# Inter-chunk and state products of the mixer in three rounded matmuls, their operands split on three engines

## Chip, cores and metric

The kernel runs on one core of one Trainium2 chip. The metric is the device time of one execution in microseconds. The engines are TensorE (PE in the rows, PEld its weight loads), VectorE (DVE), ScalarE (ACT), GpSimd (POOL) and SyncE (SP), which issues the DMAs.

## What is computed

A two-layer model on 1024 tokens of width 512: a Mamba-like mixer, a 4-bit quantised SwiGLU, a small attention over heads within a token, and a routed low-rank layer. The change is in the mixer. Its reference, cut to what matters (64 heads of 64 in 8 groups, state width 128, a causal conv of 4 taps):

```python
proj = einsum('bld,pd->blp', hidden_states, in_proj_w)      # gate, x, B, C, dt
xBC = silu(causal_conv(hbc, conv_weight) + conv_bias)       # x, B, C
dt_p = softplus(dt + dt_bias); dA = exp(dt_p * A)
def step(state, inp):
    state = state * dA_t[..., None, None] + dtx_t[..., None] * B_t[:, :, None, :]
    y_t = einsum('bhpn,bhn->bhp', state, C_t)
y = ys + x * D
yn = y * rsqrt(mean(y * y) + EPS) * norm_weight * silu(gate)  # mean over a group
x = x + einsum('bli,di->bld', yn, out_proj_w)
```

The final state is not an output of the whole program.

## The kernel before

The recurrence is computed in chunks of 128 tokens: 8 groups of heads, and in each group 8 chunks c = 0 to 7 (n = 8g + c counts them all). Per chunk, `y` is the sum of an intra-chunk part (`em`, the masked decay matrix times B and C, with `x_dt`), an inter-chunk part (C with the `state` left by the chunks before, scaled by `ecum`) and `x_d`. The state becomes its decayed self (`state_dec`) plus the state product, B with the weighted x (`x_w`).

Most products are taken with operands split into a rounded part and a rest (`_hi`, `_lo`, type fp32r): `three_pass` runs hi x hi, hi x lo and lo x hi into one PSUM bank. The inter-chunk product (L904, into `p_in`) and the state product (L909, into `p_x`) are plain fp32 matmuls, which the profile shows as two matmul records each.

Each engine has a fixed order of work written out by hand, with semaphores between them. In chunk c:
- TensorE: transposes of x into `p_x` (L872), transposes of the last chunk's z into `p_in` (L835), `p_gb` (B transposed, and B with C), the decay product into `p_d0` and `p_d1` (L888), the first conv tile into `p_tile` (L84 and L88), the output product of the last chunk into `p_y`, the inter-chunk product, the state product, in chunks 0, 1, 4 and 5 a second conv tile into `p_d1`, the intra-chunk product into `p_y` (L920), and the next chunk's gate product. It makes the conv tiles of the half sequence ahead; the last group has none from chunk 4 on, and takes the gate product in their place.
- ScalarE: the silu of a conv tile left over, `xs` from `p_x` (L471), `zt_hi` from `p_in` (L453), the exponentials `em` (L477) with a table load ahead, the read of `p_tile` into `conv` (L444), roundings of the next group's weights (L433, L436), the tile's silu (L449) with a table load, the square sum of y (L495), the silu of the gate (L459), which waits until z is done.
- VectorE: `gm` and `b_tok` from `p_gb`, `zt_lo` (L578), `em` times `gm` (L660), two taps of the conv tile (L558), the residual, which adds the last chunk's `p_y` into `x_res` (L586) and so frees `p_y`, the other taps, `y` from `p_in` (L684), the state (L690, L692), `y` plus `p_y` (L701), `z` (L710), taps of the second tile.
- GpSimd: `state_dec` (L365), `x_w` (L371), `x_dt` (L374), `g_rstd` (L401), `x_d` (L379), rests of weights `w_lo` (L407), `y` plus `x_d` (L390).

TensorE's intra-chunk product waits for `em` (`s_m`), for `x_dt` and for the residual of the chunk before (`s_res`). The inter-chunk product waits for the state (`s_stu`) and for `zt_lo` (`s_zlo`), since `p_in` holds z transposed.

```python
pe.wait_ge(s_m, 2 * (n + 1))
pe.wait_ge(s_xdt, n + 1)
wait(pe, s_res, n)
for h in range(HG):
    mm = pe.matmul(p_y[:, h * HD:(h + 1) * HD], em[:, c % 2, h * P:(h + 1) * P],
                   x_dt[:, h * HD:(h + 1) * HD], start=True, stop=True)
```

Of the kernel before, what the change touches and what calls it, by code (L numbers as in the profile page):

```python
# [14 lines left out]
F32 = mybir.dt.float32  # L15
# [8 lines left out]
P = 128  # L24
# [67 lines left out]
def mixer(nc, io, ctx, x_res, ident, mean_var2, rstd2, q_prep):  # L92
# [5 lines left out]
    def sb(name, shape, dt=F32):  # L98
        return ctx.enter_context(nc.sbuf_tensor(name, shape, dt))
# [4 lines left out]
    def sem(name):  # L104
        return ctx.enter_context(nc.semaphore(name))
# [17 lines left out]
    em = sb("em", [P, 2, HG * P])  # L123
    b_tok = sb("b_tok", [P, P])
    xs = sb("xs", [P, 2, GW])
# [57 lines left out]
        sem(f"act_{k}") for k in ("xs", "e", "cin", "xc", "sg", "zhi", "ss", "whi"))  # L183

    s_head = sem("ve_head")
    s_gm, s_m, s_tap, s_zlo, s_res, s_t, s_y, s_z, s_stu, s_v, s_wloo = (
# [52 lines left out]
    def by_head(ap):  # L239
        return ap.rearrange("p (h d) -> p h d", h=HG)  # L240
# [116 lines left out]
    def _(pool):  # L357
        def group(g, last):
            for c in range(NC):
                n = g * NC + c  # L360
                st = g * (NC - 1) + c
                if c > 0:

                    pool.wait_ge(s_stu, n)
                    pool.tensor_tensor(by_head(state_dec[:]), by_head(state[:]), heads(ETOT, c), ALU.mult)\  # L365
                        .then_inc(s_std, 1)
                if c == 0:
                    pool.wait_ge(s_head, 5 * (g + 1))
                pool.wait_ge(s_xs, n + 1)
                wait(pool, s_stn, n)  # L370
                pool.tensor_tensor(by_head(x_w[:]), by_head(xs[:, c % 2, :]), heads(DTW, c), ALU.mult)\  # L371
                    .then_inc(s_xw, 1)
                wait(pool, s_intra, n)
                pool.tensor_tensor(by_head(x_dt[:]), by_head(xs[:, c % 2, :]), heads(DT, c), ALU.mult)\  # L374
                    .then_inc(s_xdt, 1)
                if not (isinstance(g, int) and n == 0):
                    norm(n - 1, (c - 1) % 2)
                wait(pool, s_y, n)
                pool.tensor_tensor(by_head(x_d[:]), by_head(xs[:, c % 2, :]),  # L379
                                   d_g[:].unsqueeze(2).broadcast_to([P, HG, HD]), ALU.mult)\  # L380
                    .then_inc(s_xd, 1)
                splits = () if last else SPLIT_IN.get(c, ())
                for w in splits:
                    if w in POOL_LO:
                        w_rest(g + 1, w)
                if c > 0:

                    pool.wait_ge(s_t, st)
                    pool.wait_ge(s_xd, n + 1)
                    pool.tensor_tensor(y[:, c % 2, :], y[:, c % 2, :], x_d[:], ALU.add).then_inc(s_txd, 1)  # L390
# [36 lines left out]
    def _(act):  # L427
# [33 lines left out]
        def group(g, last):  # L461
            for c in range(NC):
                n = g * NC + c
                first = isinstance(g, int) and n == 0
                left, now, later = conv_tiles(g, last, c)
# [78 lines left out]
    def _(ve):  # L544
# [89 lines left out]
        def group(g, last):  # L634
# [7 lines left out]
            for c in range(NC):  # L642
# [9 lines left out]
                ve.tensor_tensor(gm, p_gb[:, 0:P], tri[:], ALU.mult).then_inc(s_gm, 1)  # L652
                ve.tensor_copy(b_tok[:], p_gb[:, P:2 * P]).then_inc(s_gm, 1)
                if not first:
                    z_rest(n - 1)
                ve.wait_ge(s_gm, 2 * (n + 1))
                for k in range(2):
# [20 lines left out]
                if c > 0:  # L678
# [6 lines left out]
                        .then_inc(s_t, 1)  # L685
                ve.wait_ge(s_stn, n + 1)
                wait(ve, s_stu, n)
                if c > 0:
                    ve.wait_ge(s_std, st)
                    ve.tensor_tensor(state[:], p_x[:], state_dec[:], ALU.add).then_inc(s_stu, 1)  # L690
                else:
                    ve.tensor_copy(state[:], p_x[:]).then_inc(s_stu, 1)  # L692
                if c == 0:
# [122 lines left out]
    def _(pe):  # L816
# [44 lines left out]
        def group(g, last):  # L861
            for c in range(NC):
# [5 lines left out]
                if c % CH == 0:  # L868
                    pe.wait_ge(s_xc, (2 * g + c // CH + 1) * TILES - 2)
                wait(pe, s_stu, n)  # L870
                for j in range(GW // P):
# [28 lines left out]
                if c > 0:  # L900

                    pe.wait_ge(s_stu, n)
                    pe.wait_ge(s_zlo, n)
                    pe.matmul(p_in[:], xbc[:, TC, cs], state[:], start=True, stop=True).then_inc(s_inter, 1)  # L904

                pe.wait_ge(s_gm, 2 * (n + 1))
                pe.wait_ge(s_xw, n + 1)
                pe.wait_ge(s_xs, n + 1)
                pe.matmul(p_x[:], b_tok[:], x_w[:], start=True, stop=True).then_inc(s_stn, 1)  # L909

# [987 lines left out]
```

## Time and profile before

| | |
|---|---|
| median of 3 runs | 1382.21 us (1380.33 to 1383.5) |
| the profiled execution | 1379.14 us, its span 1377.3 us |
| busy share of the span | TensorE 94%, VectorE 67%, ScalarE 49%, GpSimd 41% |
| the mixer's groups | from about 66 us to about 1012 us, 119.4 us a group |
| granted TensorE clock in a middle group | 1.00 |

In a middle group the transposes of x mark the chunks: chunk 0 starts at 542.95, chunk 1 at 558.29, chunk 2 at 575.04, chunk 3 at 588.64, chunk 4 at 602.08, chunk 5 at 618.32, chunk 6 at 634.55, chunk 7 at 648.00, and the next group at 662.34. All rows below of such a stretch are of this group. In the rows a time is the start in us from the span's start, then the duration; what stands in brackets is the engine's idle time before the instruction and what ended it. Matmul records overlap, so that the time of a matmul is read from the distance of the starts.

### The profile page before, as it was taken

How to read it: one execution, taken by the hardware profiler on the slowest of the kernel's cores; microseconds unless marked ns; L12 is line 12 of the kernel's file. 1: busy time of each engine (PE TensorE's matmuls, PEld its weight loads, DVE VectorE, ACT ScalarE, POOL GpSimd, SP SyncE). 2: the span in 40 equal slices, each digit the busy share in tenths (PEclk: the TensorE clock that was granted, in tenths of full speed). 3: DMA queues.
4: the chain of work that ended last, by engine and by line, in shares of the span. 5: the costliest groups of instructions: out<-in, count | busy, mean ns of one | idle time of the engine just before them, and what ended most of it. 6: DMA issues, size and time to landing. Idle time of an engine off the chain costs nothing. (4 is left out here: it accounts for less than half of the span.)

```text
span 1377.3 us, 20717 instructions
## 1 busy us (share of the span) xinstructions
PE 1294.3 (94%) x6278; PEld 1011.8 (73%) x6278; DVE 926.7 (67%) x1764; ACT 675.7 (49%) x1055; POOL 564.0 (41%) x567
## 2 busy tenths in 40 slices
PE   5699999999999999999999999999869999879986
PEld 4577877877887787788788778778646766667764
DVE  5876677667667766766766676676656445368995
ACT  3465565566556556656655566655323223222220
POOL 2145345444544534444454444434433333333331
PEclk9899999999999999999999999999979999999997
DMA  5111011011101101100200120000013222131200
GB/s 150 59 47 33 1 59 36 17 33 47 31 1 63 31 16 32 54 24 1 70 24 16 32 62 16 6 28 3 8 41 115 84 77 80 49 100 29 58 16 23
DMA packets 44248, 57.61 MB, mean 42 GB/s; under 512 B 10182, under 2 KB 21156, under 8 KB 43922
## 3 DMA queue, kind: packets, MB, share of 16 engines
q1 hardware_dynamic: 44178, 56.84, 13.7%
q8 instruction: 23, 0.38, 0.1%
q14 instruction: 47, 0.39, 0.1%
HBM read 49.87 MB, written 6.96 MB: 41 GB/s over the span
## 5 line engine op out<-in xcount | busy, mean ns | idle before, releaser
L371 POOL TENSOR_TENSOR x_w<-xs,head_g 128x512 f32<-128x512 f32 x64 | 66.8, 1044 | 296.7 <-ACT xs L471 271.9
L558 DVE SCALAR_TENSOR_TENSOR conv<-p_tile,conv_taps,conv 128x511 f32<-128x511 f32 x189 | 140.7, 745 | 31.7 <-ACT conv L444 22.0
L920 PEld LDWEIGHTS p_y<-x_dt,em 128*128 128x128 f32 x1024 | 123.5, 192 | 26.1 <-issue 22.9
L390 POOL TENSOR_TENSOR y<-y,x_d 128x512 f32<-128x512 f32 x56 | 71.8, 1282 | 165.9 <-DVE y L684 165.9
L660 DVE TENSOR_TENSOR em<-em,p_gb 128x512 f32<-128x512 f32 x128 | 82.2, 683 | 73.6 <-ACT em L477 73.6
L920 PE MATMUL p_y<-x_dt,em 128*128 128x64 f32 x1024 | 121.8, 272 | 4.5 <-DVE x_res L586 4.4
L449 ACT ACTIVATE xbc<-conv 128x512 f32<-128x512 f32 x96 | 60.3, 628 | 130.3 <-DVE conv L566 73.7
L84 PE MATMUL p_tile<-xn_hi,w_hi 128*128 128x512 f32 x252 | 111.2, 441 | 3.2 <-DVE halo L562 3.2
L495 ACT ACTIVATE junk<-y 128x512 f32<-128x512 f32 x64 | 40.5, 633 | 144.3 <-DVE y L701 130.8
L558 DVE SCALAR_TENSOR_TENSOR conv<-p_d,conv_taps,conv 128x511 f32<-128x511 f32 (+2 forms) x99 | 73.9, 746 | 50.7 <-ACT conv L444 46.8
L84 PE MATMUL p_gate<-w_hi,xn_hi 128*128 128x512 f32 x256 | 106.1, 415 | 1.1 <-ACT gate L459 1.1
L84 PE MATMUL p_y<-w_hi,zt_hi 128*128 128x512 f32 x256 | 102.5, 400 | 2.2 <-ACT zt_hi L453 2.2
L407 POOL TENSOR_TENSOR w_lo<-w_raw,w_hi 128x512 fp32r<-128x512 f32 x64 | 82.8, 1309 | 52.5 <-ACT w_hi L433 52.5
L84 PE MATMUL p_y<-w_lo,zt_hi 128*128 128x512 f32 x256 | 102.4, 400 | 0.0
L84 PE MATMUL p_gate<-w_lo,xn_hi 128*128 128x512 f32 x256 | 100.3, 392 | 0.0
L84 PE MATMUL p_tile<-xn_lo,w_hi 128*128 128x512 f32 x252 | 99.3, 394 | 0.0
L477 ACT ACT_TABLE_LOAD x64 | 82.1, 1283 | 1.2
L449 ACT ACT_TABLE_LOAD x61 | 78.3, 1283 | 1.1
L365 POOL TENSOR_TENSOR state_dec<-state,head_g 128x512 f32<-128x512 f32 x56 | 58.4, 1043 | 33.2 <-DVE state L692 33.2
L88 PE MATMUL p_y<-w_hi,zt_lo 128*128 128x512 f32 x256 | 71.1, 400 | 0.0
L1095 POOL TENSOR_TENSOR f_w_lo<-wf,f_w_hi 128x512 fp32r<-128x512 f32 x22 | 30.2, 1374 | 99.7 <-ACT f_w_hi L1136 99.7
L477 ACT ACTIVATE em<-p_d 128x512 f32<-128x512 f32 x128 | 69.6, 596 | 0.7
(293 smaller groups left out, 3316.0 us busy)
## 6 DMA issues: line engine op xcount, KB each, us to landing
w_raw<-w SPq DMA_DIRECT2D x112, 256.0 KB, 2.9
q_words<-q SPq DMA_DIRECT2D x33, 256.0 KB, 2.7
h_ring<-h_lo_rows SPq DMA_DIRECT2D x6, 704.0 KB, 5.0
h_lo_rows<-h_rest SPq DMA_DIRECT2D x11, 256.0 KB, 2.0
x_res<-x SPq DMA_DIRECT2D x8, 256.0 KB, 4.9
out<-out_t SPq DMA_DIRECT2D x8, 256.0 KB, 2.3
h_lo_rows<-h_rest SPq DMA_DIRECT2D x11, 128.0 KB, 1.9
decay_lhs<-cum_parts SPq DMA_DIRECT2D x64, 6.0 KB
```

The lines of the kernel that those rows point to most:

```text
L84: pe.matmul(out, lhs(k)[0], rhs(k)[n], start=(start and k == 0 and n == 0), stop=False)
L88: last = pe.matmul(out, lhs(k)[1], rhs(k)[0], start=False, stop=(k == k_tiles - 1))
L365: pool.tensor_tensor(by_head(state_dec[:]), by_head(state[:]), heads(ETOT, c), ALU.mult)\
L371: pool.tensor_tensor(by_head(x_w[:]), by_head(xs[:, c % 2, :]), heads(DTW, c), ALU.mult)\
L390: pool.tensor_tensor(y[:, c % 2, :], y[:, c % 2, :], x_d[:], ALU.add).then_inc(s_txd, 1)
L407: pool.tensor_tensor(w_lo[:, w, :], w_raw[:, w % RAW, :], w_hi[:, w, :].bitcast(F32), ALU.subtract)\
L449: act.activation(xbc[:, j, half_cols(hf)], conv[:, j % 2, :], ACT.Silu).then_inc(s_xc, 1)
L477: act.activation(em[:, c % 2, k * 512:(k + 1) * 512], p[:], ACT.Exp).then_inc(s_e, 1)
L495: act.activation(junk[:], y[:, c % 2, :], ACT.Square, accum_out=ss[:, c % 2:c % 2 + 1])\
L558: ve.scalar_tensor_tensor(out=conv[:, s, sh:], in0=p[:, 0:HALF - sh], scalar=conv_w[:, bass.ds(g, 1), j, tap], in1=conv[:, s, sh:], op0=AL ...
L660: ve.tensor_tensor(m, m, gm.unsqueeze(1).broadcast_to([P, HG // 2, P]), ALU.mult)\
L920: mm = pe.matmul(p_y[:, h * HD:(h + 1) * HD], em[:, c % 2, h * P:(h + 1) * P], x_dt[:, h * HD:(h + 1) * HD], start=True, stop=True)
```

## The change

The operands of the two products are split into a rounded part and a rest, and each product becomes a `three_pass` of one tile. C and the state and the weighted x are rounded by ScalarE (`c_hi`, `st_hi` behind `zt_hi` and ahead of the exponentials; `xw_hi` behind them), B by VectorE, in place of the copy `b_tok`. The rests are made by GpSimd (`c_lo` ahead of `x_dt`, `xw_lo` behind `g_rstd` and ahead of `x_d`) and VectorE (`b_lo` and `st_lo`, ahead of `em` times `gm`). A group's eighth chunk makes no `x_w`, no state product and no new state, since the next group begins with its own; so chunk 7 of a group no longer decays the state for the chunk behind it either, and the counts of the semaphores follow. The core of the diff:

```diff
--- GpSimd
-                if c > 0:
-                    pool.wait_ge(s_stu, n)
+                if 0 < c < NC - 1:
+                    pool.wait_ge(s_stu, st)
                     pool.tensor_tensor(by_head(state_dec[:]), by_head(state[:]), heads(ETOT, c), ALU.mult)\
                         .then_inc(s_std, 1)
...
+                if c > 0:
+                    pool.wait_ge(s_chi, st)
+                    pool.tensor_tensor(c_lo[:], xbc[:, TC, c * P:(c + 1) * P], c_hi[:].bitcast(F32), ALU.subtract)\
+                        .then_inc(s_clo, 1)
                 wait(pool, s_intra, n)
                 pool.tensor_tensor(by_head(x_dt[:]), by_head(xs[:, c % 2, :]), heads(DT, c), ALU.mult)\
                     .then_inc(s_xdt, 1)
                 if not (isinstance(g, int) and n == 0):
                     norm(n - 1, (c - 1) % 2)
+                if c < NC - 1:
+                    pool.wait_ge(s_xwhi, st + 1)
+                    pool.tensor_tensor(xw_lo[:], x_w[:], xw_hi[:].bitcast(F32), ALU.subtract).then_inc(s_xwlo, 1)
--- ScalarE
                 if not first:
                     z_round(n - 1)
+                if c > 0:
+                    wait(act, s_inter, st - 1)
+                    act.wait_ge(s_xc, (2 * g + c // CH + 1) * TILES)
+                    act.activation(c_hi[:], xbc[:, TC, c * P:(c + 1) * P], ACT.Copy).then_inc(s_chi, 1)
+                    act.wait_ge(s_stu, st)
+                    act.activation(st_hi[:], state[:], ACT.Copy).then_inc(s_sthi, 1)
...
                 for k, p in enumerate((p_d0, p_d1)):
                     act.activation(em[:, c % 2, k * 512:(k + 1) * 512], p[:], ACT.Exp).then_inc(s_e, 1)
+                if c < NC - 1:
+                    act.wait_ge(s_xw, st + 1)
+                    wait(act, s_stn, st)
+                    act.activation(xw_hi[:], x_w[:], ACT.Copy).then_inc(s_xwhi, 1)
--- VectorE
-                ve.tensor_copy(b_tok[:], p_gb[:, P:2 * P]).then_inc(s_gm, 1)
+                ve.tensor_copy(b_hi[:], p_gb[:, P:2 * P]).then_inc(s_gm, 1)
                 if not first:
                     z_rest(n - 1)
-                ve.wait_ge(s_gm, 2 * (n + 1))
+                ve.wait_ge(s_gm, 3 * n + 2)
+                ve.tensor_tensor(b_lo[:], p_gb[:, P:2 * P], b_hi[:].bitcast(F32), ALU.subtract).then_inc(s_gm, 1)
+                if c > 0:
+                    ve.wait_ge(s_sthi, st)
+                    ve.tensor_tensor(st_lo[:], state[:], st_hi[:].bitcast(F32), ALU.subtract).then_inc(s_stlo, 1)
+                ve.wait_ge(s_gm, 3 * (n + 1))
--- TensorE
-                    pe.wait_ge(s_stu, n)
+                    for done in (s_chi, s_clo, s_sthi, s_stlo):
+                        pe.wait_ge(done, g * (NC - 1) + c)
                     pe.wait_ge(s_zlo, n)
-                    pe.matmul(p_in[:], xbc[:, TC, cs], state[:], start=True, stop=True).then_inc(s_inter, 1)
-
-                pe.wait_ge(s_gm, 2 * (n + 1))
-                pe.wait_ge(s_xw, n + 1)
-                pe.wait_ge(s_xs, n + 1)
-                pe.matmul(p_x[:], b_tok[:], x_w[:], start=True, stop=True).then_inc(s_stn, 1)
+                    three_pass(pe, p_in[:], lambda k: (c_hi[:], c_lo[:]), lambda k: (st_hi[:], st_lo[:]), 1)\
+                        .then_inc(s_inter, 1)
+
+                if c < NC - 1:
+                    pe.wait_ge(s_gm, 3 * (n + 1))
+                    pe.wait_ge(s_xwlo, g * (NC - 1) + c + 1)
+                    pe.wait_ge(s_xs, n + 1)
+                    three_pass(pe, p_x[:], lambda k: (b_hi[:], b_lo[:]), lambda k: (xw_hi[:], xw_lo[:]), 1)\
+                        .then_inc(s_stn, 1)
```

## Rows read from the trace of the kernel before

**Rows 1.** Windows, chunks 2, 3, 4 and 7: length, each engine's busy time, clock, DMA

```profile
core 0: us, PE busy (x) PEld busy (x) DVE busy (x) ACT busy (x) POOL busy (x), PEclk, DMA share, GB/s
...
575.04:588.64 13.60, 13.60 (x71) 10.74 (x70) 9.78 (x21) 8.80 (x14) 8.37 (x8) 1.00 0.15 39
588.64:602.08 13.44, 13.44 (x70) 10.75 (x69) 8.97 (x19) 7.99 (x14) 7.14 (x7) 1.00 0.00 1
602.08:618.32 16.24, 16.24 (x83) 13.00 (x82) 9.67 (x17) 8.66 (x13) 7.15 (x7) 1.00 0.12 34
...
648.00:662.34 14.34, 13.70 (x71) 10.66 (x70) 9.22 (x16) 9.44 (x15) 7.42 (x7) 1.00 0.24 75
```

**Rows 2.** Timeline, where TensorE waits in chunks 1 and 7

```profile
560.01 0.61 PE L888 MATMUL p_d<-decay_rhs,decay_lhs 90*128 90x512 bf16 x2 [0.35 <-DVE conv L566]
...
656.82 0.74 DVE L586 SCALAR_TENSOR_TENSOR x_res<-p_y,g_rstd,x_res 128x512 f32<-128x512 f32 x1
...
657.71 1.97 PE L920 MATMUL p_y<-x_dt,em 128*128 128x64 f32 x16 [0.64 <-DVE x_res L586]
```

**Rows 3.** Timeline of ScalarE in chunk 2

```profile
576.36 0.63 ACT L449 ACTIVATE xbc<-conv 128x512 f32<-128x512 f32 x1 [0.53 <-DVE conv L566]
...
579.28 1.09 ACT L477 ACTIVATE em<-p_d 128x512 f32<-128x512 f32 x2
580.25 0.79 ACT L444 ACTIVATE conv<-p_tile,conv_taps 128x512 f32<-128x512 f32 x1
```

**Rows 4.** Timeline of VectorE in chunk 2

```profile
581.36 1.64 DVE L558 SCALAR_TENSOR_TENSOR conv<-p_tile,conv_taps,conv 128x511 f32<-128x511 f32 x2 [0.17 <-issue]
582.92 0.74 DVE L586 SCALAR_TENSOR_TENSOR x_res<-p_y,g_rstd,x_res 128x512 f32<-128x512 f32 x1
```

**Rows 5.** Timeline of TensorE in chunk 2

```profile
581.45 1.10 PE L88 MATMUL p_y<-w_hi,zt_lo 128*128 128x512 f32 x4
582.38 1.02 PE L904 MATMUL p_in<-state,xbc 128*128 128x512 f32 x2
583.24 1.02 PE L909 MATMUL p_x<-x_w,b_tok 128*128 128x512 f32 x2
584.10 1.90 PE L920 MATMUL p_y<-x_dt,em 128*128 128x64 f32 x16
```

**Rows 6.** Groups of instructions by form, whole span: busy, mean ns, idle before

```profile
L407 POOL TENSOR_TENSOR w_lo<-w_raw,w_hi 128x512 fp32r<-128x512 f32 x64 | 82.8, 1309 | 52.5 <-ACT w_hi L433 52.5
...
L477 ACT ACTIVATE em<-p_d 128x512 f32<-128x512 f32 x128 | 69.6, 596 | 0.7
...
L433 ACT ACTIVATE w_hi<-w_raw 128x512 fp32r<-128x512 f32 x80 | 46.2, 627 | 2.0 <-DMA w_raw<-w 2.0
...
L1547 ACT ACTIVATE hw_hi<-t_p_t 128x128 fp32r<-128x128 f32 x8 | 2.2, 277 | 15.1 <-PE t_p_t L1723 15.1
```

**Rows 7.** Timeline, chunk 3 and chunk 6

```profile
593.36 0.78 ACT L444 ACTIVATE conv<-p_tile,conv_taps 128x512 f32<-128x512 f32 x1 [0.55 <-PE p_tile L88]
...
596.03 0.75 DVE L586 SCALAR_TENSOR_TENSOR x_res<-p_y,g_rstd,x_res 128x512 f32<-128x512 f32 x1
...
597.54 1.67 PE L920 MATMUL p_y<-x_dt,em 128*128 128x64 f32 x14
...
638.15 1.09 ACT L477 ACTIVATE em<-p_d 128x512 f32<-128x512 f32 x2
639.28 0.78 ACT L444 ACTIVATE conv<-p_tile,conv_taps 128x512 f32<-128x512 f32 x1
...
641.94 0.75 DVE L586 SCALAR_TENSOR_TENSOR x_res<-p_y,g_rstd,x_res 128x512 f32<-128x512 f32 x1
...
643.46 1.78 PE L920 MATMUL p_y<-x_dt,em 128*128 128x64 f32 x15
```

**Rows 8.** Timeline, intra-chunk product in chunk 6 of the last group; all waits for L586

```profile
994.57 1.97 PE L920 MATMUL p_y<-x_dt,em 128*128 128x64 f32 x16 [0.19 <-DVE x_res L586]
...
  DVE x_res L586: 4.4, 8
```

More of the change, by code:

```diff
@@ L123, in mixer @@
     em = sb("em", [P, 2, HG * P])
-    b_tok = sb("b_tok", [P, P])
+    b_hi, b_lo = sb("b_hi", [P, P], F32R), sb("b_lo", [P, P], F32R)
+    c_hi, c_lo = sb("c_hi", [P, P], F32R), sb("c_lo", [P, P], F32R)
+    st_hi, st_lo = sb("st_hi", [P, GW], F32R), sb("st_lo", [P, GW], F32R)
+    xw_hi, xw_lo = sb("xw_hi", [P, GW], F32R), sb("xw_lo", [P, GW], F32R)
     xs = sb("xs", [P, 2, GW])
@@ L183, in mixer @@
         sem(f"act_{k}") for k in ("xs", "e", "cin", "xc", "sg", "zhi", "ss", "whi"))
+    s_chi, s_sthi, s_xwhi = (sem(f"act_{k}") for k in ("chi", "sthi", "xwhi"))
+    s_clo, s_xwlo, s_stlo = sem("pool_clo"), sem("pool_xwlo"), sem("ve_stlo")
     s_head = sem("ve_head")
@@ L369, in group @@
                 pool.wait_ge(s_xs, n + 1)
-                wait(pool, s_stn, n)
-                pool.tensor_tensor(by_head(x_w[:]), by_head(xs[:, c % 2, :]), heads(DTW, c), ALU.mult)\
-                    .then_inc(s_xw, 1)
+                if c < NC - 1:
+                    wait(pool, s_stn, st)
+                    pool.tensor_tensor(by_head(x_w[:]), by_head(xs[:, c % 2, :]), heads(DTW, c), ALU.mult)\
+                        .then_inc(s_xw, 1)
+                if c > 0:
+                    pool.wait_ge(s_chi, st)
+                    pool.tensor_tensor(c_lo[:], xbc[:, TC, c * P:(c + 1) * P], c_hi[:].bitcast(F32), ALU.subtract)\
+                        .then_inc(s_clo, 1)
                 wait(pool, s_intra, n)
@@ L463, in group @@
                 n = g * NC + c
+                st = g * (NC - 1) + c
                 first = isinstance(g, int) and n == 0
@@ L685, in group @@
                         .then_inc(s_t, 1)
[L686 to L692, printed above, removed]
+                if c < NC - 1:
+                    ve.wait_ge(s_stn, st + 1)
+                    wait(ve, s_stu, st)
+                    if c > 0:
+                        ve.wait_ge(s_std, g * (NC - 2) + c)
+                        ve.wait_ge(s_stlo, st)
+                        ve.tensor_tensor(state[:], p_x[:], state_dec[:], ALU.add).then_inc(s_stu, 1)
+                    else:
+                        wait(ve, s_stlo, st)
+                        ve.tensor_copy(state[:], p_x[:]).then_inc(s_stu, 1)
                 if c == 0:
@@ L869, in group @@
                     pe.wait_ge(s_xc, (2 * g + c // CH + 1) * TILES - 2)
-                wait(pe, s_stu, n)
+                if c > 0:
+                    pe.wait_ge(s_stu, g * (NC - 1) + c)
+                else:
+                    wait(pe, s_xs, n)
                 for j in range(GW // P):
@@ L900, in group @@
                 if c > 0:
-                    pe.wait_ge(s_stu, n)
+                    for done in (s_chi, s_clo, s_sthi, s_stlo):
+                        pe.wait_ge(done, g * (NC - 1) + c)
                     pe.wait_ge(s_zlo, n)
-                    pe.matmul(p_in[:], xbc[:, TC, cs], state[:], start=True, stop=True).then_inc(s_inter, 1)
-                pe.wait_ge(s_gm, 2 * (n + 1))
-                pe.wait_ge(s_xw, n + 1)
-                pe.wait_ge(s_xs, n + 1)
-                pe.matmul(p_x[:], b_tok[:], x_w[:], start=True, stop=True).then_inc(s_stn, 1)
+                    three_pass(pe, p_in[:], lambda k: (c_hi[:], c_lo[:]), lambda k: (st_hi[:], st_lo[:]), 1)\
+                        .then_inc(s_inter, 1)
+                if c < NC - 1:
+                    pe.wait_ge(s_gm, 3 * (n + 1))
[3 more added lines that the diff above has]
+                        .then_inc(s_stn, 1)
                 if later:
```

## The prediction

> **What bounds the kernel now.** I read the windows first, one for each of the eight chunks of a middle group. TensorE is busy for all of 13.44 us in chunk 3 and all of 16.24 us in chunk 4; in chunk 7 it works 13.70 of 14.34. VectorE works 9.0 to 9.8 us of these chunks, ScalarE 8.0 to 9.4, GpSimd 7.1 to 8.4 [rows 1]. So in the mixer TensorE sets the time. The waits show who stands close behind it. In chunk 1 the decay product waits 0.35 us for VectorE's conv taps, in chunk 7 the intra-chunk product waits 0.64 us for VectorE's residual (L586) [rows 2]. That second wait is a rule for later: the residual ends at 656.82 + 0.74 = 657.56 and the product starts at 657.71, so intra starts 0.15 us after the residual's end whenever TensorE is there earlier.
>
> Behind the residual lies one chain through two engines, seen best in chunk 2. ScalarE goes without a hole from the silu at 576.36 through xs, zt_hi, the table load and the exponentials to reading p_tile at 580.25 [rows 3]. VectorE's first two taps wait for that read and start at 581.36, the residual follows at 582.92 and ends at 583.66 [rows 4], and the intra product starts at 584.10 [rows 5]. The slack is 584.10 - 583.66 - 0.15 = 0.29 us.
>
> **The products.** The four last matmuls of the output product run from 581.45 to the start of L904 at 582.38, so a rounded matmul of 512 columns takes 0.93/4 = 0.233 us. The fp32 product takes 583.24 - 582.38 = 0.86, and L909 takes 584.10 - 583.24 = 0.86 [rows 5]. Three rounded ones take 0.70: each product gains 0.16. There are 56 inter-chunk and 64 state products; 8 state products go, worth 0.86 each. If TensorE stayed the bound the sum would be 112 x 0.16 + 8 x 0.86 = 24.8 us gained. The trace has the 0.233 for the same operand form, so I take it.
>
> The Trainium skill (FP8 and Floating Point Precision, TensorE Precision Notes) counts a true fp32 product as four passes through the array. By its count three passes cost 3/4 of 0.86 = 0.645 and the same sum would be 31 us. The measured spacing of the three decides, since it also holds the loads between them, and the sum here goes by 0.70.
>
> **The splits.** ScalarE gets three copies in a chunk. A w_hi copy from SBUF lasts 0.627 and two exponentials in a row take 1.09, where each lasts 0.596, so neighbours overlap by 0.10: st_hi and xw_hi cost 0.52 each on the queue. The 128-column copy hw_hi lasts 0.277 from PSUM [rows 3, 6]; c_hi reads SBUF, which adds 0.03, so 0.20. Bounds of c_hi are 0.17 and 0.28. All three stand between zt_hi and the reading of p_tile: c_hi and st_hi ahead of the table load, xw_hi behind the exponentials. That is 1.24 us in one chain (0.72 in chunk 7, which has no xw_hi, and in chunk 0 the 0.52 of xw_hi alone, which I take to lie in the time in which the queue waits for p_tile, as chunk 3 has 0.55 of it [rows 7]).
>
> VectorE gets b_lo (0.2) and st_lo (0.7). They lie in the 1.2 us in which it waits for the exponentials; no cost, and if that cover went, the taps would slip by their length. GpSimd gets c_lo (some 0.35) ahead of x_dt and xw_lo, which I take at the 1.31 of w_lo [rows 6]. In chunk 2 xw_lo would start behind xw_hi, at 579.28 + 0.72 + 0.97 + 0.60 = 581.6, and end at 582.9; the state product would want it at 582.38 + 0.70 = 583.08. It is in time with 0.15 to spare, and in chunk 1 with about as little: cost nothing, at worst 0.3 in each of those. No DMA is added, and w_raw's splits behind xw_lo on GpSimd end before they are missed.
>
> **What a group then takes**, by chunk, "d" being the decay product's start:
> - Chunk 0 to the d of chunk 2: chunk 0's 0.16 goes into chunk 1's wait for taps, which VectorE sets. Chunk 1 gains 0.32; its left tile's taps follow by 0.25. Sum -0.25.
> - Chunk 2: the residual slips by the full 1.24, to an end at 584.90; intra starts at 585.05 in place of 584.10. +0.95.
> - Chunk 3: z follows the residual through the taps, y and GpSimd's y without slack, so it is 1.24 late, and so is the gate's silu, which waits for z; with the three copies the read of p_tile (593.36, idle 0.55 before it) slips by 1.24 + 1.24 less 0.66 of room (the 0.55 and the overlap of 0.11 that an instruction which waits loses) = 1.82, and the residual from 596.03 with it. It ends at 598.59 and intra starts at 598.74 where it was 597.54: +1.20, that is +0.25 over chunk 2 [rows 7].
> - Chunks 4 and 5 have a second conv tile, 12 matmuls of 0.233, between the state product and intra, so the residual has 2.8 us to spare: -0.32 each.
> - Chunk 6: from the exponentials to the read of p_tile it is 639.28 - 638.15 = 1.13, where it is 580.25 - 579.28 = 0.97 in chunk 2, so ScalarE has 0.16 of slack, the residual slips by 1.08 from 641.94 to an end of 643.76, and intra goes from 643.46 to 643.91. +0.45 [rows 3, 7].
> - Chunk 7: the residual already sets intra. It slips by 0.72 less the same 0.66 of room before p_tile: +0.06. The dropped state product (0.86) is lost in the same wait.
> Sum: -0.25 + 0.95 + 0.25 - 0.64 + 0.45 + 0.06 = +0.82 us a group, 5.7 for seven groups.
>
> The last group has no splits of weights and, from chunk 4 on, no taps. Its chunks 0 to 3 come to +0.4, chunk 4 to -0.3, chunk 5 to 0; in chunk 6 the intra product waits for the residual behind a row of small VectorE steps (994.57, idle 0.19) [rows 8], which start behind the exponentials, so +0.7, and chunk 7 likewise +0.7. Sum +1.5. After the mixer nothing changes.
>
> **Total:** 5.7 + 1.5 = +7.2 us. On the profiled execution (1379.14 us, span 1377.3) that is 1386.3; on the median of 1382.21, which lies 3.1 above it, 1389.4.
>
> **The rivals.**
> - *TensorE stays the bound (the other side).* ScalarE is busy only 8 to 9 of 13.5 us [rows 1], so the three copies could fall into its idle time. For it: the products do get shorter by 24.8. Against it: the idle time lies after the read of p_tile, while the copies lie before it. What would remain lost are chunk 0's 0.16 and chunk 7's 1.02, 1.2 x 7 = 8.3, so -16.5 and 1366 us. The place that decides is the read of p_tile: if it slips by less than about 0.9 in place of 1.24, the group's sum turns negative.
> - *Half way.* The read slips by about 0.9 to 1.0 (c_hi nearly free, or a residual that needs less than 0.15 to release intra): chunks 2, 3 and 6 lose what 1, 4 and 5 gain, and the time stays within 0.2% at about 1382.
> - *The state product waits too.* xw_lo runs ScalarE, GpSimd, TensorE in a row, with margins of 0.15 us in chunks 1 and 2 and 0.3 in chunk 0. If GpSimd is 0.5 late there, chunk 1 carries 0.35 on into the taps and chunk 0 and 3 add 0.3 each. About +1 a group more: some +14 us in all, 1396.
> - *Split without effect on the path:* chunk 7's state product alone cannot give the gain, since intra waits for the residual there.
>
> **Chances.** The forecast (+7) 0.60, TensorE bound 0.12, half way 0.13, xw_lo late 0.15. About 0.2% (2.8 us) is what a measurement of this kernel can tell from no change. The forecast's own range goes from +3 (c_hi at its lower bound, 0.15 of release that vanishes) to +12 (c_hi at 0.28 and chunks 1 and 2 paying 0.3): 1385 to 1394. The range must take in most of the slower rival and part of the half way case: 1376 to 1398. Faster 0.14, same 0.14, slower 0.72.
>
> **What would show it.** L904 and L909 should show three matmuls, 0.70 from the first to the next product. ScalarE should read p_tile some 5.9 us after the transposes of chunks 5 and 6 where it now takes 4.7. Chunks 2 and 3 should take about 14.5 and 13.7 (13.60 and 13.44 now), chunks 4 and 5 15.9, and the wait of the intra product for L586, 4.4 us in all now [rows 8], should grow to some 25 to 30 us. If those chunks stay at 13.1 and the wait hardly grows, the chain was read wrongly; if L909's start waits for xw_lo, the third rival holds.

## The result and the profile after

The change makes the kernel slower: 1411.17 us as the median of 5 runs (1407.07 to 1413.05) against 1382.21. The ratio by the runs of both kernels is 1.0219 [1.0203, 1.0234]; the two medians alone give 1.0210. The forecast was 1389.4 with a range of 1376 to 1398. The sign is right, and the loss, 29 us, is four times the 7 forecast.

The profiled execution has a span of 1411.1 us where the one before had 1377.3. It is the slowest of the five, so what follows accounts for 33.8 us and not for 29. The windows of the same middle group show where the loss lies. Columns as in [rows 1].

```profile
core 0: us, PE busy (x) PEld busy (x) DVE busy (x) ACT busy (x) POOL busy (x), PEclk, DMA share, GB/s
560.84:576.04 15.20, 15.20 (x82) 12.80 (x80) 11.44 (x26) 9.80 (x15) 5.90 (x6) 1.00 0.01 1
576.04:592.73 16.69, 16.16 (x85) 13.28 (x84) 14.03 (x28) 11.93 (x20) 10.52 (x10) 1.00 0.28 95
592.73:607.99 15.26, 13.59 (x73) 10.95 (x72) 11.01 (x23) 9.44 (x15) 10.15 (x10) 1.00 0.14 35
607.99:622.24 14.25, 13.56 (x72) 11.01 (x71) 9.94 (x21) 9.18 (x16) 9.56 (x10) 1.00 0.01 1
622.24:638.35 16.11, 16.10 (x84) 13.34 (x83) 11.33 (x21) 10.35 (x18) 9.29 (x10) 1.00 0.13 33
638.35:654.23 15.88, 15.88 (x84) 13.36 (x83) 11.30 (x22) 9.79 (x16) 8.00 (x8) 1.00 0.00 1
654.23:668.13 13.90, 13.34 (x73) 11.03 (x72) 9.79 (x20) 9.01 (x15) 7.00 (x7) 1.00 0.01 1
668.13:684.11 15.98, 14.25 (x69) 11.85 (x68) 10.16 (x17) 10.05 (x17) 7.28 (x7) 0.89 0.21 67
```

Against the chunks before (15.34, 16.75, 13.60, 13.44, 16.24, 16.23, 13.45, 14.34) the eight differ by -0.14, -0.06, +1.66, +0.81, -0.13, -0.35, +0.45 and +1.64 us, +3.88 in all. The forecast had -0.25 for chunks 0 and 1 (up to the decay product of chunk 2), +0.95, +0.25, -0.32, -0.32, +0.45 and +0.06, in all +0.82. Chunks 4 to 6 are as forecast or close to it. Chunks 2, 3 and 7 are not, and in chunk 7 the eighth column stands out: the granted clock is 0.89.

**Chunk 7.** TensorE's timeline there, to be set beside [rows 2]:

```profile
677.89 2.68 PE L959 MATMUL p_y<-x_dt,em 128*128 128x64 f32 x16 [1.73 <-DVE x_res L610]
...
680.90 0.63 PE L84 MATMUL p_gate<-w_lo,xn_hi 128*128 128x512 f32 x1
...
682.96 0.39 PE L84 MATMUL p_gate<-w_lo,xn_hi 128*128 128x512 f32 x1
```

The intra product starts 677.89 - 668.13 = 9.76 us after the chunk's transposes, where it was 657.71 - 648.00 = 9.71 [rows 1, 2]: the +0.05 is the forecast's +0.06. The wait is 1.73 us now, with the state product gone and the inter-chunk one shorter. What follows was not forecast. The same matmuls are longer after the wait (2.68 us for the sixteen that took 1.97, 0.63 for one that takes 0.39). Windows of one microsecond show why:

```profile
678.00:679.00 1.00, 1.00 (x10) 1.00 (x11) 0.95 (x3) 0.37 (x1) 0.00 (x0) 0.98 0.78 211
679.00:680.00 1.00, 1.00 (x7) 1.00 (x6) 0.30 (x1) 0.26 (x1) 0.62 (x1) 0.50 0.52 193
...
681.00:682.00 1.00, 1.00 (x4) 0.81 (x3) 0.97 (x2) 0.53 (x1) 0.00 (x0) 0.50 0.00 0
682.00:683.00 1.00, 1.00 (x5) 0.78 (x5) 0.17 (x1) 0.20 (x2) 0.00 (x0) 0.82 0.02 8
```

The wait ends at 677.89. From about a microsecond later the granted clock is 0.50, which is 1.2 GHz of the 2.4, for some three microseconds. Of the seven groups that are followed by another, five show a chunk 7 of 15.9 to 16.0 us, two one of 17.57 (clock 0.81), where the low clock lasts twice as long.

**Chunks 1 and 2.** Here are rows of VectorE and GpSimd in the second half of chunk 1, first of the kernel before, then of the changed one:

```profile
565.46 2.52 POOL L407 TENSOR_TENSOR w_lo<-w_raw,w_hi 128x512 fp32r<-128x512 f32 x2 [0.51 <-ACT w_hi L433]
...
568.18 0.73 DVE L566 SCALAR_TENSOR_TENSOR conv<-halo,conv_taps,conv 128x3 f32<-128x3 f32 x3
```

```profile
585.52 2.54 POOL L420 TENSOR_TENSOR w_lo<-w_raw,w_hi 128x512 fp32r<-128x512 f32 x2
...
587.17 1.42 DVE L590 SCALAR_TENSOR_TENSOR conv<-halo,conv_taps,conv 128x3 f32<-128x3 f32 x3
...
588.63 0.63 ACT L462 ACTIVATE xbc<-conv 128x512 f32<-128x512 f32 x1 [2.44 <-DVE conv L590]
...
594.71 0.61 PE L923 MATMUL p_d<-decay_rhs,decay_lhs 90*128 90x512 bf16 x2 [0.61 <-DVE conv L590]
```

L590 (L566 before) is the three short halo taps, of 3, 2 and 1 columns. They take 1.42 us here, and 0.74 for the next tile of the same kernel (593.91), where GpSimd is idle. They start at 587.17 while GpSimd's pair of w_lo runs until 585.52 + 2.54 = 588.06. The view of a shorter stretch (587.3 to 588.0) shows the second w_lo and the first tap alone:

```profile
586.77 1.29 POOL L420 TENSOR_TENSOR w_lo<-w_raw,w_hi 128x512 fp32r<-128x512 f32 x1
...
587.17 0.91 DVE L590 SCALAR_TENSOR_TENSOR conv<-halo,conv_taps,conv 128x3 f32<-128x3 f32 x1
```

The first tap lasts until 588.08, 0.02 us after the end of w_lo, and the other two take their usual 0.22 each. The same happens late in chunk 2 (603.91, 1.37 us). Behind the taps the tile's silu is 1.93 us later in its chunk than before (588.63 - 576.04 against 568.95 - 558.29), ScalarE's read of the second tile then follows without a wait, 0.57 later, and the decay product of chunk 2, which did not wait before, waits 0.61 us.

ScalarE's queue in chunk 2 is what [rows 3] became. First two rows of the kernel before that [rows 3] leaves out, then the changed kernel:

```profile
577.38 0.59 ACT L453 ACTIVATE zt_hi<-p_in 128x512 fp32r<-128x512 f32 x1
577.99 1.28 ACT L477 ACT_TABLE_LOAD   x1
```

```profile
595.70 0.59 ACT L466 ACTIVATE zt_hi<-p_in 128x512 fp32r<-128x512 f32 x1
596.17 0.31 ACT L491 ACTIVATE c_hi<-xbc 128x128 fp32r<-128x128 f32 x1
596.38 0.63 ACT L493 ACTIVATE st_hi<-state 128x512 fp32r<-128x512 f32 x1
597.02 1.28 ACT L497 ACT_TABLE_LOAD   x1
...
599.29 0.64 ACT L501 ACTIVATE xw_hi<-x_w 128x512 fp32r<-128x512 f32 x1
599.81 0.78 ACT L457 ACTIVATE conv<-p_tile,conv_taps 128x512 f32<-128x512 f32 x1
```

From zt_hi to the table load it is 1.32 us where it was 0.61, so c_hi and st_hi add 0.71; from xw_hi to L457 it is 0.52. The forecast had 0.72 and 0.52. The waits over the whole span, and the groups by form, which answer to [rows 8] and [rows 6], with two groups of the kernel before ahead of them:

```profile
PE p_y L959 <- DVE x_res L610: 27.9, 31, 2.2
...
PE p_d L923 <- DVE conv L590: 7.7, 15, 0.6
```

```profile
L374 POOL TENSOR_TENSOR x_dt<-xs,head_g 128x512 f32<-128x512 f32 x64 | 66.8, 1044 | 0.0
...
L566 DVE SCALAR_TENSOR_TENSOR conv<-halo,conv_taps,conv 128x3 f32<-128x3 f32 x48 | 10.7, 222 | 1.7
```

```profile
L384 POOL TENSOR_TENSOR x_dt<-xs,head_g 128x512 f32<-128x512 f32 x64 | 88.4, 1381 | 0.0
...
L590 DVE SCALAR_TENSOR_TENSOR conv<-halo,conv_taps,conv 128x3 f32<-128x3 f32 x48 | 20.7, 432 | 1.7
```

The three-column tap, the first of each three, went from 222 to 432 ns on average (the two-column and one-column ones stay at 221 and 220), and x_dt, an unchanged GpSimd instruction, from 1044 to 1381. Both grow where the two engines work at one time on operands in SBUF.

### The profile page after: what moved, and what is told of

It is laid out like the page before. It is cut to its first block and busy times, and to the rows that moved or that the text cites. A ratio compares the mean times of both kernels' runs of the same rounds, so it can differ in the third digit from the quotient of the medians.

```text
span 1411.1 us, 21653 instructions
## 1 busy us (share of the span) xinstructions
PE 1296.2 (92%) x6364; PEld 1040.0 (74%) x6374; DVE 988.3 (70%) x1876; ACT 740.6 (52%) x1223; POOL 668.3 (47%) x663
## 5 line engine op out<-in xcount | busy, mean ns | idle before, releaser
L377 POOL TENSOR_TENSOR x_w<-xs,head_g 128x512 f32<-128x512 f32 x56 | 58.6, 1046 | 253.8 <-ACT xs L485 253.8
L959 PE MATMUL p_y<-x_dt,em 128*128 128x64 f32 x1024 | 127.4, 279 | 27.9 <-DVE x_res L610 27.9
L84 PE MATMUL p_gate<-w_hi,xn_hi 128*128 128x512 f32 x256 | 113.0, 442 | 1.1 <-ACT gate L472 1.1
L84 PE MATMUL p_gate<-w_lo,xn_hi 128*128 128x512 f32 x256 | 106.5, 416 | 0.0
L390 POOL TENSOR_TENSOR xw_lo<-x_w,xw_hi 128x512 fp32r<-128x512 f32 x56 | 72.5, 1295 | 39.8 <-ACT xw_hi L501 39.8
L384 POOL TENSOR_TENSOR x_dt<-xs,head_g 128x512 f32<-128x512 f32 x64 | 88.4, 1381 | 0.0
L1134 POOL TENSOR_TENSOR f_w_lo<-wf,f_w_hi 128x512 fp32r<-128x512 f32 x22 | 30.3, 1376 | 100.6 <-ACT f_w_hi L1175 100.6
L88 PE MATMUL p_gate<-w_hi,xn_lo 128*128 128x512 f32 x256 | 70.6, 398 | 0.0
```

Source lines behind the costliest of these rows:

```text
L84: pe.matmul(out, lhs(k)[0], rhs(k)[n], start=(start and k == 0 and n == 0), stop=False)
L88: last = pe.matmul(out, lhs(k)[1], rhs(k)[0], start=False, stop=(k == k_tiles - 1))
L390: pool.tensor_tensor(xw_lo[:], x_w[:], xw_hi[:].bitcast(F32), ALU.subtract).then_inc(s_xwlo, 1)
```

## The experiments

The theory had three parts, each with its price a group: ScalarE's copies delay the residual (+1.0, as forecast); the clock falls after the wait that chunk 7 leaves (1.6 or 3.2); the halo taps and GpSimd's w_lo, both on operands in SBUF, stand in each other's way (+1.2; "the port" in the expectations and below). The rivals were that the time went with the missing state product alone, or that the whole loss was ScalarE's chain. All ratios are to the kernel before, which ran again beside each set of experiments. Its medians there are 1379.2 to 1380.4 us where it had 1382.2 at first, so a difference in us between kernels of different sets can be 1 to 3 us off; the ratios are not touched by that.

**e1: fill chunk 7.** Two unused copies of the state product stand where TensorE would wait.

```diff
+                else:
+                    pe.wait_ge(s_gm, 3 * (n + 1))
+                    pe.wait_ge(s_xs, n + 1)
+                    for _ in range(2):
+                        three_pass(pe, p_x[:], lambda k: (b_hi[:], b_lo[:]), lambda k: (xw_hi[:], xw_lo[:]), 1)
```

> The changed kernel with six rounded 512-column matmuls (1.4 us, their result unused) on TensorE in each group's eighth chunk, between the inter-chunk and the intra-chunk product, where TensorE now waits 1.73 us for the residual. The end of that wait is set by VectorE's residual and does not move. Clock theory: the long wait is what lets the granted clock fall to 0.5 behind it (0.89 or 0.81 over chunk 7), which costs 1.6 or 3.2 us a group; with the hole filled chunk 7 goes from 15.98 to about 14.4 us and the kernel is 12 to 15 us faster than the changed one, some 1397. Rival (the eighth chunk is long because of VectorE and the residual alone): no change, 1411.

Measured: 1400.17 us, 1.0142 [1.0121, 1.0163], near the 1397 expected. More work, 11 us less time. Chunk 7 in the windows:

```profile
658.97:673.35 14.38, 14.02 (x75) 11.59 (x74) 10.15 (x17) 10.04 (x17) 7.32 (x7) 1.00 0.23 74
```

It takes 14.27 to 14.39 in all seven groups at clock 1.00, so the clock is worth 1.6 us a group (15.98 less 14.38), and 3.2 in two of them. The gain is less than the 14.4 that this adds up to, because in four groups chunk 2 takes 16.83 to 16.85 in place of 15.25 (one group of the changed kernel shows that, 16.85): there the clock is 0.90, and the wait for the residual ahead of it is 1.05 us.

**e2: only the missing state product.** The kernel before, without x_w, state product and state update in a group's eighth chunk, the counts of the semaphores adapted. The core of it:

```diff
-                pe.matmul(p_x[:], b_tok[:], x_w[:], start=True, stop=True).then_inc(s_stn, 1)
+                if c < NC - 1:
+                    pe.matmul(p_x[:], b_tok[:], x_w[:], start=True, stop=True).then_inc(s_stn, 1)
```

> The kernel before with one part of the change alone: no weighted x, state product and new state in a group's eighth chunk; both products stay fp32. TensorE's wait in chunk 7 grows from 0.64 to about 1.5 us. Clock theory: a wait of that length lets the clock fall too, chunk 7 becomes about 1.6 us longer and the kernel 8 to 12 us slower, 1390 to 1394. Rival (the dropped product only lengthens a wait that is there anyway): within 0.1 us a group, 1382; second rival (it saves TensorE time): 5 us faster.

Measured: 1383.04 us, 1.0016 [1.0000, 1.0031]. The wait for the residual is 1.5 us in chunk 7, but the clock falls in two of seven groups only (17.51 and 15.94 us; 14.08 to 14.34 in the others):

```profile
528.31:545.82 17.51, 16.01 (x68) 12.77 (x67) 9.35 (x21) 9.44 (x15) 6.38 (x6) 0.81 0.20 62
```

So dropping 0.86 us of work gains nothing, and by itself costs little. The expectation of 8 to 12 us took the fall for certain in each group, and was too high for that.

**e3: c_hi and st_hi one chunk earlier.** ScalarE makes them for the next chunk in the time in which it waits for y.

```diff
-                if c > 0:
-                    wait(act, s_inter, st - 1)
...
-                    act.activation(st_hi[:], state[:], ACT.Copy).then_inc(s_sthi, 1)
...
+                if c < NC - 1:
+                    wait(act, s_inter, st)
+                    act.wait_ge(s_xc, (2 * g + (c + 1) // CH + 1) * TILES)
+                    act.activation(c_hi[:], xbc[:, TC, (c + 1) * P:(c + 2) * P], ACT.Copy).then_inc(s_chi, 1)
+                    act.wait_ge(s_stu, st + 1)
+                    act.activation(st_hi[:], state[:], ACT.Copy).then_inc(s_sthi, 1)
                 act.wait_ge(s_y, n + 1)
```

> The changed kernel with ScalarE's roundings of C and of the state (c_hi, st_hi) made one chunk ahead, where ScalarE waits for y, in place of between zt_hi and the exponentials. Chain theory (my prediction's): the read of p_tile comes 0.72 us earlier in chunks 2, 3 and 6, the residual too, the wait of the intra product for it shrinks from 27.9 us to under 12, and the kernel is 1.5 to 2.5 us a group faster, 12 to 20 in all, since some clock drops go as well. Rival (VectorE and GpSimd hold each other up and set the taps): the read moves but the residual does not, under 4 us.

Measured: 1390.03 us, 1.0068 [1.0045, 1.0090], 21 us less than the changed kernel, and the wait for the residual goes from 27.9 to:

```profile
PE p_y L959 <- DVE x_res L610: 15.8, 15, 1.7
```

Chunks 2, 3 and 6 take 13.95, 13.64 and 13.19 us. With chunk 6 below its 13.45 of before, the copies ahead of the table load are what delayed it. The wait stays above the 12 us expected, since chunk 7 keeps 1.68 of it in each middle group, and the clock does not fall less often, as was expected: chunk 7 takes 15.69 to 17.52 us in six of seven groups, and 14.34 in the one without a fall. So the 21 us came from ScalarE's chain and what hangs on it, not from the clock.

**e4: the halo taps read PSUM.** The short taps take their columns from the tile in PSUM in place of the halo in SBUF, so that only one input lies in SBUF. These few columns of the conv are then computed from other data: the kernel measures a price and is no replacement.

```diff
-                    ve.scalar_tensor_tensor(out=conv[:, s, 0:sh], in0=halo[:, j, tap:],
+                    ve.scalar_tensor_tensor(out=conv[:, s, 0:sh], in0=p[:, 0:sh],
```

> The changed kernel with the three short taps at the half's seam (three columns each) reading their first operand from PSUM in place of the saved halo in SBUF, so that this part of the conv is computed from other data. Nothing else moves. Shared-port theory: these taps lasted 0.22 us in the kernel before and the first of them 0.43 on average in the changed one (0.9 where GpSimd's w_lo runs), since an instruction with two SBUF operands waits for GpSimd to finish; with one SBUF operand they are back at 0.22, chunk 1's taps end 0.65 earlier, the decay product of chunk 2 starts 0.5 us earlier, and the kernel is about 0.5 to 1.2 us a group faster, 4 to 10 in all. Rival (VectorE is late by its own added work): they are short again, but the time stays within 2 us.

Measured: 1395.83 us, 1.0116 [1.0085, 1.0146], 15 us less. The taps of chunk 1 beside w_lo, the group by form, and the wait:

```profile
573.27 1.28 POOL L420 TENSOR_TENSOR w_lo<-w_raw,w_hi 128x512 fp32r<-128x512 f32 x1
...
573.67 0.73 DVE L590 SCALAR_TENSOR_TENSOR conv<-p_tile,conv_taps,conv 128x3 f32<-128x3 f32 x3
```

```profile
L590 DVE SCALAR_TENSOR_TENSOR conv<-p_tile,conv_taps,conv 128x3 f32<-128x3 f32 x32 | 7.1, 221 | 1.1
```

```profile
PE p_d L923 <- DVE conv L590: 3.6, 8, 0.5
```

All three taps now lie within w_lo's 573.27 to 574.55 and take 0.73 together, 221 ns each, and the decay product's wait goes from 7.7 to 3.6 us. Chunks 2 and 3 take 14.64 and 13.59, so 1.3 us a group is the price. The gain is above the 4 to 10 expected, since the clock falls less often as well: chunk 7 takes 15.96 and 14.38 us in turn from group to group, behind the same wait of 1.73 us. That pair is a second measure of the clock's 1.6 us, within one execution and with nothing else changed.

**e5 and e6: the residual first.** VectorE's two w_lo rests of chunk 7 go behind the residual, in the changed kernel (e5) and in the one before (e6).

```diff
-                else:
-                    for w in SPLIT_IN.get(c, ()):
-                        if w in VE_LO:
-                            w_rest(g + 1, w)
                 for tile in now:
                     tile_taps(*tile, range(2))
                 if not first:
                     residual(n - 1, (c - 1) % NC)
+                if not last:
+                    for w in SPLIT_IN.get(c, ()):
+                        if w in VE_LO:
+                            w_rest(g + 1, w)
```

> The changed kernel with one move on VectorE: the residual of the chunk before goes ahead of the rests of the next group's weights in a group's eighth chunk. That takes two instructions of 0.65 us from ahead of the residual. Clock theory: TensorE's wait there falls from 1.73 to about 0.5 us, too short for the clock to fall, and the product starts 1.3 earlier: chunk 7 goes from 15.98 to about 13.2 us, and with what chunk 2 still loses the kernel is at 1.005 to 1.009 of the one before. Rival (the clock falls for another reason than that wait): chunk 7 still shows 0.89, and only 1.3 us a group is gained, 1.015.

> The kernel before with the same move. TensorE's wait of 0.64 us in chunk 7 goes, and the records give 14.34 - 13.45 = 0.9 us a group: 6 us faster, ratio 0.9955. Rival (the late weights' rests then hold up the gate product of the next group): no change.

Measured: e5 1404.57 us, 1.0181 [1.0163, 1.0200]; e6 1383.57 us, 1.0025 [1.0014, 1.0036], slower than the kernel before. Both expectations missed. Chunk 7 gets shorter (13.75 and 13.73, the clock stays at 1.00 in e5 too), but the next chunk 0 gets longer: 16.4 to 17.0 for 15.20 in e5, and 16.5 for 15.34 in e6. The timeline of e5:

```profile
669.25 2.96 POOL L420 TENSOR_TENSOR w_lo<-w_raw,w_hi 128x512 fp32r<-128x512 f32 x2 [1.65 <-ACT w_hi L446]
...
670.12 2.63 DVE L618 TENSOR_TENSOR w_lo<-w_raw,w_hi 128x512 fp32r<-128x512 f32 x2
670.36 1.97 PE L959 MATMUL p_y<-x_dt,em 128*128 128x64 f32 x16 [0.26 <-DVE x_res L610]
...
677.26 0.65 PE L867 MATMUL p_in<-identity,z 128*128 128x128 f32 x4 [0.84 <-DVE z L742]
```

The rests, 688 ns each where they stood, take 2.63 for two beside GpSimd's w_lo, and GpSimd's pair 2.96 where alone it takes 2.5: each engine holds the other up. What was won before the intra product is paid behind it, through y and z.

**e7 and e8: all moves together.** e3, e5, and xw_hi behind the reading of p_tile; e8 with e4's taps too.

```diff
-                if c < NC - 1:
-                    act.wait_ge(s_xw, st + 1)
...
                 for T, tg, j, _ in now:
                     tile_in(T, tg, j)
+                if c < NC - 1:
+                    act.wait_ge(s_xw, st + 1)
```

> The changed kernel with three moves and no work less: c_hi and st_hi one chunk ahead, xw_hi behind the read of p_tile, the residual ahead of the weights' rests in chunk 7. ScalarE's read of p_tile is then where it was in the kernel before. Chain theory: chunks 3, 6 and 7 come to 13.1 to 13.3 us, chunk 2 to 13.5, chunk 5 to 15.9, a group to some 117 us in place of 119.4, and the kernel to 1362 to 1368, ratio about 0.988. Rival (the port that VectorE and GpSimd share and the longer row to xw_lo take it back): 1378 or more.

> The kernel with the three moves and also the three short taps reading their first operand from PSUM, so that this part of the conv is computed from other data. It gives the price of the shared port where ScalarE is no longer in the way. Port theory: in chunk 1 or 2 these taps still meet GpSimd's w_lo, so another 0.3 to 0.6 us a group goes, 2 to 4 us. Rival (with the moves nothing waits for them): within 1 us of the kernel with the moves.

Measured: e7 1394.67 us, 1.0109 [1.0091, 1.0128]; e8 1380.68 us, 1.0001 [0.9988, 1.0015]. In e7 the residual hardly holds TensorE any more, and z does in its place:

```profile
PE p_in L867 <- DVE z L742: 21.9, 24, 1.5
...
PE p_y L959 <- DVE x_res L610: 3.5, 9, 1.5
```

VectorE starts earlier and meets more of GpSimd's work: the three-column tap takes 501 ns on average and the two-column one 508. With the taps in PSUM (e8) 14 us come back, far more than the 2 to 4 expected. e7's expectation fell, and the rival on the port held, though the port is only about half of it: e8 is still 13 us above the 1368 that e7 was to reach at most. In the middle groups its chunk 0 takes 15.7 to 17.0 us, with waits for xw_lo and in four of them for z, and in three groups chunk 7 takes 15.29 to 15.32 at clock 0.89, behind two short waits:

```profile
658.43 1.97 PE L959 MATMUL p_y<-x_dt,em 128*128 128x64 f32 x16 [0.26 <-DVE x_res L610]
661.03 0.49 PE L84 MATMUL p_gate<-w_hi,xn_hi 128*128 128x512 f32 x1 [0.63 <-DVE w_lo L618]
```

e7 has the same two waits in each of its middle groups, and its clock stays at 1.00 in chunk 7.

**e9: fill chunk 7 and make the copies early** (e1 and e3 together).

> The changed kernel with the six filling matmuls of chunk 7 and with c_hi and st_hi one chunk ahead. Both theories together: the chunks of the kernel with early roundings stay (13.95, 13.64, 13.19 for chunks 2, 3 and 6) and chunk 7 loses its clock drops (14.35 in place of 14.34 to 17.52), which takes 14 us from that kernel's profile: 1374 to 1376, ratio 0.995 to 0.998. Rival (the clock then falls in other waits): 1.000 or more.

Measured: 1375.10 us, 0.9977 [0.9963, 0.9990]. As expected, and the fastest kernel here that computes all of the reference, though by a quarter of a per cent only. Against e3 the filling takes chunk 7 to 14.33 or 14.35 in every middle group and 15 us off the time. Its chunks 2 and 3 take 13.94 and 13.66, and chunk 7:

```profile
644.01:658.34 14.33, 14.01 (x76) 11.60 (x74) 9.41 (x17) 9.44 (x15) 7.34 (x7) 1.00 0.22 74
```

**e10 and e11: the halo taps from PSUM in both** (e1 with e4; e9 with e4), so that a few columns of the conv come from other data in these too.

> The changed kernel with the filling matmuls and with the short taps' first operand from PSUM (that part of the conv is computed from other data); c_hi and st_hi stay where the change puts them. Port theory: chunks 2 and 3 come to 14.6 and 13.6, without a clock drop in chunk 2, whose wait is shorter: 9 to 12 us faster than with the filling matmuls alone, ratio 1.006 to 1.008. What is left over the kernel before is ScalarE's chain alone. Rival: as with the filling matmuls, 1.014.

> All three: filling matmuls, c_hi and st_hi a chunk ahead, short taps from PSUM (that part of the conv is computed from other data). With ScalarE's chain, the port and the clock out of the way only the shorter products and xw_hi's 0.52 are left: 117.5 to 118 us a group, 1366 to 1369, ratio 0.990 to 0.993. Rival (a further hold that no run has shown): 0.997 or more.

Measured: e10 1394.62 us, 1.0106 [1.0087, 1.0124]; e11 1371.45 us, 0.9945 [0.9925, 0.9965]. Middle groups take 120.4 us in e10 and 118.1 in e11, where e1 has 121.6 (without the low clock in chunk 2), e9 118.8 and the kernel before 119.4. So the taps cost 1.2 us a group where ScalarE's copies make them late, and 0.7 where they don't: the prices are not independent of each other. e11 stays a little short of the 0.990 to 0.993 expected, e10 more so of its 1.006 to 1.008. In one group of e10 the clock falls in chunk 2 after all (16.21 us), and at the mixer's end it falls more often: the last group takes 99.2 us where e1's takes 97.0. The 15 us behind the last chunk's transposes, first e1, then e10:

```profile
1015.28:1030.28 15.00, 10.23 (x56) 7.72 (x55) 9.22 (x17) 7.54 (x14) 5.25 (x6) 0.94 0.05 6
```

```profile
1006.97:1021.97 15.00, 12.51 (x55) 9.73 (x55) 9.21 (x17) 7.39 (x13) 4.91 (x6) 0.73 0.03 4
```

**e12: another way to part the two engines.** e9 with the short taps behind y and state on VectorE, reading their halo from SBUF as the reference needs it.

```diff
                 for tile in now:
-                    tile_taps(*tile, range(2, TAPPED[tile[3]]))
+                    tile_taps(*tile, range(2, 3))
...
+                for tile in now:
+                    tile_taps(*tile, range(3, TAPPED[tile[3]]))
                 if c == 0:
                     w_rest(g, TILES + KT)
```

> The kernel with filling matmuls and early roundings, the taps from their right data, and one swap on VectorE: the three short taps of the first tile go behind y and the new state in place of ahead of them. GpSimd's w_lo has then ended and GpSimd's y starts earlier. Port theory: the taps are back near 0.22, a group takes about 117.5 to 118.3 us and the kernel 1368 to 1372, ratio 0.992 to 0.995. Rival (they meet GpSimd's y instead, or y's place does not matter): like the kernel without the swap, 0.997.

Measured: 1400.49 us, 1.0157 [1.0136, 1.0178], a clear miss. Timeline of chunk 1 and the wait it causes:

```profile
579.81 1.28 POOL L403 TENSOR_TENSOR y<-y,x_d 128x512 f32<-128x512 f32 x1
580.02 2.34 DVE L590 SCALAR_TENSOR_TENSOR conv<-halo,conv_taps,conv 128x3 f32<-128x3 f32 x3
...
581.04 1.04 POOL L370 TENSOR_TENSOR state_dec<-state,head_g 128x512 f32<-128x512 f32 x1
...
588.47 0.60 PE L925 MATMUL p_d<-decay_rhs,decay_lhs 90*128 90x512 bf16 x2 [1.33 <-DVE conv L590]
```

Behind y the taps meet GpSimd's y and state_dec, released by what VectorE has just done. Three instructions on six columns take 2.34 us, and start 2.2 us later in the chunk than in e9 too. The decay product waits 20.8 us in all where it waited 3.6 in e9.

A halo kept in spare columns of a PSUM bank, which would give e11 the right data, wasn't tried.

## Why the prediction was wrong

*The products* were right. In the timeline of chunk 2 the inter-chunk product has its three matmuls at 600.70, 600.92 and 601.15 and the state product the next at 601.38: 0.68 to 0.70 each. Chunk 5, where nothing else moved, gained 0.35 where 0.32 was forecast. *The splits on ScalarE* were right to about 0.01: the read of p_tile comes 5.82 us after the transposes in chunks 5 and 6 where it came after 4.73 (+1.09; the forecast for chunk 6 was +1.08), chunk 6 pays exactly the forecast 0.45, and the wait for the residual is 27.9 us in all where 25 to 30 was said. e3 shows it by undoing it.

*The sum by groups was right once both missed mechanisms are out.* e10 has neither the low clock in chunk 7 nor the port's part in the taps. Its middle group is 120.4 - 119.4 = +1.0 us (the forecast had +0.82), with chunks 2, 3 and 6 at 14.64, 13.57 and 13.91: +1.04, +0.13 and +0.46 for a forecast of +0.95, +0.25 and +0.45. The first group, which the forecast took to be like the others, pays nothing (118.33 after 118.36), so the seven come to +6.2 for a forecast of 5.7.

*The step that failed first* is chunk 7's "+0.06. The dropped state product (0.86) is lost in the same wait." The intra product's start is right to 0.01, but the wait grew from 0.64 to 1.73 us and what comes behind it ran at half clock. The step priced a hole in TensorE's work at its length only. By the chunks of the changed kernel against those of e1, the low clock costs 1.6 us in five groups, 3.2 in two, and 0.8 net in the one chunk 2: 15.2 us of the 33.8 by which the spans differ. e1 shows it by filling the hole, e9 against e3 shows it again, and e4 by its groups with and without a fall. No rival had it.

*The second* is "w_raw's splits behind xw_lo on GpSimd end before they are missed", with "no cost" for what VectorE gets. They are not missed by TensorE, but they stand in VectorE's way. Counted from the transposes, the halo taps of chunk 1 start at 587.17 - 576.04 = 11.13, 1.24 later than before, just as ScalarE's chain says. GpSimd's w_lo ends at 12.02 where it ended at 9.7: it slipped by 2.3, since c_lo, xw_lo and a longer x_dt stand ahead of it. Before, w_lo was done 0.2 us before the taps; now they start in its midst, and the first of them lasts until it ends. The price is the difference of e1's and e10's groups: 121.6 - 120.4 = 1.2 us in six groups, 119.9 - 118.3 = 1.6 in the first, 8.8 in all.

The Trainium skill (SBUF — State Buffer, SBUF: two separate sides) says that a VectorE operation with both inputs in SBUF and a GpSimd operation that reads SBUF exclude each other for the whole instruction. By that rule the cost depends on what the tiny operation meets and not on its size, and these traces agree: the three-column tap takes 222 ns alone, 432 on average in the changed kernel (909 in chunk 1, until w_lo's end), 559 in e12, and 221 again with one input in PSUM. That what they share is a port is the page's account; the runs show the waiting, not the port.

*The last group* was forecast at +1.5. Its first seven chunks take 1.7 more (97.00 after 95.28), nearly all of it in chunk 6 (14.85 after 13.17, where +0.7 was forecast): the wait for the residual there is 2.22 us where it was 0.19. Behind the last chunk's transposes, where chunk 7 was forecast at +0.7, lie another 0.9. That makes +2.6 in all; why chunk 6 pays 1.7 and not 0.7 was not followed up.

Sum: 6.2 for ScalarE's chain and the shorter products in seven groups, 15.2 for the clock, 8.8 for the port and 2.6 in the last group make 32.8 of the 33.8 in the profiled spans. Of the rest 0.6 lies ahead of the mixer's first transposes.

*The rivals.* "TensorE stays the bound" did not come, and the sign it named is plain: the read of p_tile slipped by 1.09 us in chunks 5 and 6, not by less than 0.9; the half-way case (0.9 to 1.0) is out by the same number. e11 shows what it takes to get near it: ScalarE's early copies, no hole in chunk 7 and no meeting of the taps with GpSimd, three edits for 0.55%, and the third at the price of wrong data. "xw_lo late" did not come either: in chunk 2 of the changed kernel the state product starts 0.23 after the last inter-chunk matmul (601.15, 601.38), without a wait. That chunk 7's dropped state product alone gives no gain was said among the rivals, and e2 bears it out (1.0016); what it can cost was not.

Not settled is what decides whether the clock falls: the same wait in the same chunk is followed by a fall in some groups and not in others, and two short waits are in three groups of e8 and in none of e7.

## What to carry to other kernels

Work taken off an engine in front of a wait that stays makes the wait longer and no more; on TensorE the longer wait can then lower the clock for the work behind it, so that filling it with unused matmuls made the changed kernel 0.8% faster. Before moving small operations on VectorE or adding any on GpSimd, lay the two timelines over each other and ask which two-input operations will now overlap, however small: the place counts, not the size, and every reordering on VectorE here (e5, e6, e7, e12) moved the collision elsewhere. Copies that split an operand belong in the time in which their engine waits anyway, a step early, and not just ahead of the instruction that the others wait for.

## What the hardware showed that was not expected

- A wait of TensorE of little over a microsecond can be followed by half the granted clock, at 1.6 or 3.2 us a time in chunk 7. In the six middle groups of each kernel a wait of 1.73 us in chunk 7 was followed by a fall in six (the changed kernel) and in three (e4), one of 1.68 us in five (e3), one of 1.5 us in two (e2), one of 1.05 us in chunk 2 in one (the changed kernel), four (e1), one (e10) and none (e4), and one of 0.64 us in none (the kernel before). Waits of 0.26 and 0.63 us, 2.0 us apart, were followed by one in three (e8) and in none (e7).
- VectorE's three instructions on 3, 2 and 1 columns took 1.42 us beside a GpSimd instruction that ended 0.89 us after their start, and 0.74 without it. The first one bore all of it (0.91 us for 0.22) and ended 0.02 us after the GpSimd instruction.
- GpSimd pays too: x_dt, unchanged, went from 1044 to 1381 ns on average over its 64 instructions, 1.50 us where st_lo ran beside it (chunk 2).
